# A graph attention kernel: the first stage's work is spread anew, and q's low half is cut strip by strip on GpSimd

## The reference, cut to what matters

```python
h = jnp.maximum(_layernorm(x), 0.0)                  # x: 4096 x 128
# layer 0
q, k, v = h @ Wq.T + bq, h @ Wk.T + bk, h @ Wv.T + bv
scores = jnp.where(adj > 0, q @ k.T / sqrt(128), -9e15)   # adj: 4096 x 4096 int32
x = x + elu(softmax(scores) @ v)
# layer 1
h = jnp.maximum(_layernorm(x), 0.0)
g = h @ W
e = leaky_relu((g @ a[:128])[:, None] + (g @ a[128:])[None, :], 0.01)
x = x + g + softmax(jnp.where(adj > 0, e, -9e15)) @ h
```

## Time and profile before

| | us |
|---|---|
| median of three executions | 794.09 |
| the profiled execution | 794.8 |
| its span | 793.0 |
| TensorE busy (matmuls) | 745.1 (94%) |
| VectorE | 582.4 (73%) |
| ScalarE | 560.0 (71%) |
| GpSimd | 365.7 (46%) |
| mean granted clock of TensorE | 0.974 |

### The profile page before, as it was taken

One profiled execution on the slowest core, in us unless ns is written; L12 is line 12 of the kernel. 1 busy time (PEld: TensorE's weight loads), 2 busy tenths in 40 slices (PEclk: granted clock), 3 DMA queues, 4 the chain that ended last, 5 costly groups with the idle time before them and its releaser, 6 DMA issues. The chain is left out here.

```text
span 793.0 us, 18058 instructions
## 1 busy us (share of the span) xinstructions
PE 745.1 (94%) x6229; PEld 629.7 (79%) x6229; DVE 582.4 (73%) x1231; ACT 560.0 (71%) x1095; POOL 365.7 (46%) x317
## 2 busy tenths in 40 slices
PE   4977999999999999999999998694999999999997
PEld 3555888888888888888888887473888888888886
DVE  4847788888788888888787886488674775685582
ACT  5936667676777768686777768484967977977911
POOL 1068587878878787878878772244000000000000
PEclk9989999999999999999999999788899999999999
DMA  6059888879787888978797842460133343333100
GB/s 225 1 183 255 265 200 242 237 211 230 214 259 201 257 219 234 239 209 233 211 256 205 254 118 41 96 132 0 32 72 82 89 76 83 88 83 89 36 10 12
DMA packets 155532, 122.47 MB, mean 154 GB/s; under 512 B 136545, under 2 KB 143201, under 8 KB 147297
## 3 DMA queue, kind: packets, MB, share of 16 engines
q1 hardware_dynamic: 154752, 121.66, 57.8%
q10 hardware_dynamic: 576, 0.26, 0.1%
q0 software_dynamic: 160, 0.00, 0.0%
HBM read 69.47 MB, written 18.87 MB: 111 GB/s over the span
## 5 line engine op out<-in xcount | busy, mean ns | idle before, releaser
L1333 PE MATMUL ps_x<-v,big 128*128 128x258 bf16 x2048 | 232.2, 275 | 2.3 <-issue 2.3
L1333 PEld LDWEIGHTS ps_x<-v,big 128*128 128x128 fp8e4 x2048 | 199.0, 98 | 32.6 <-issue 2.4
L679 DVE CUSTOM_DVE_ANT_0 scores<-ps_s,mask_neg 128x1024 f32<-128x1024 f32 x128 | 156.0, 1219 | 8.2 <-PE ps_s L766 8.2
L600 ACT ACTIVATE scores<-scores,neg_max 128x1024 f32<-128x1024 f32 x128 | 146.1, 1144 | 12.7 <-DVE neg_max L685 12.2
L537 POOL TENSOR_SCALAR mask_bytes<-adj_sb 128x2048 uint8<-128x2048 int32 x64 | 121.0, 1908 | 44.9 <-POOLq L79 39.9
L607 ACT ACTIVATE pT_high<-ps_t 128x512 bf16<-128x512 f32 x128 | 76.1, 595 | 91.4 <-PE ps_t L780 90.6
L874 ACT ACTIVATE big<-s_block,s_col 128x512 fp8e4<-128x512 f32 x224 | 139.6, 722 | 0.0
L698 DVE TENSOR_TENSOR low<-scores 128x1024 bf16<-128x1024 f32 x64 | 113.0, 1765 | 28.5 <-ACT scores L600 23.5
L552 POOL TENSOR_SCALAR mask_neg<-mask_bytes 128x2048 bf16<-128x2048 uint8 x64 | 126.7, 1979 | 5.4 <-POOL mask_bytes L537 0.4
L764 PE MATMUL ps_s<-k_hi,q_strip 128*128 128x512 f32 x256 | 113.1, 442 | 6.5 <-DVE row_max L679 4.2
L766 PE MATMUL ps_s<-k_hi,q_strip 128*128 128x512 f32 x256 | 102.2, 399 | 0.0
(11 more groups left out here) (139 smaller groups left out, 1059.2 us busy)
## 6 DMA issues: line engine op xcount, KB each, us to landing
adj_sb<-in_adj SPq DMA_DIRECT2D x64, 1024.0 KB, 6.4
mask_bytes_dram<-mask_bytes SPq DMA_DIRECT2D x32, 512.0 KB, 3.0
x_sb<-in_x SPq DMA_DIRECT2D x8, 256.0 KB, 6.0
out<-res SPq DMA_DIRECT2D x32, 64.0 KB, 1.5
lowT<-low SPq DMA_TRANSPOSE x64, 5.2
big<-mask_bytes_dram SPq DMA_TRANSPOSE x32, 4.5
raw_w<-in_L_gnn_Wq ACTq DMA_DIRECT2D x1, 64.0 KB, 3.4
raw_w<-in_L_gnn_Wk ACTq DMA_DIRECT2D x1, 64.0 KB, 4.2
```

The lines of the kernel that those rows point to most:

```text
L600: nc.scalar.activation(sc, sc, ACT.Exp, bias=neg_max[:, bn:bn + 1], accum_out=row_sum[:, bn, k:k + 1]).then_inc(exp_done, 1)
L679: nc.vector.tensor_tensor_reduce(out=scores[bn % 2][:, part(k)], in0=ps_s[k % 2][:], in1=mask[bn % 2][:, part(k)], scale=1.0, scalar=LOWES ...
L1333: last = nc.tensor.matmul(ps_x[b % 2][k][:], by_key_tile(m, t)[:, b], v1[k][:, t, :].bitcast(BF16), start=(t == 0), stop=(t == T - 1))
```

## The change

1. The first stage is a block of its own, no longer `norm_and_project`. GpSimd normalises three tiles of each chunk, ScalarE the fourth. Only k is split in high and low there; q becomes one f32 tile, `q_sb`. The first strips of q are cut in it, and GpSimd makes strip 0's bytes between the chunks and its mask behind them.
2. The v products, `hT` kept for them, move to the attention loop's block, ahead of period 0, in `ps_t` between the first scores of strips 0 and 1.
3. In the loop, ScalarE copies the high half of a strip of q (`q_high_strip`), and GpSimd subtracts it from `q_sb` for the low half (`q_low_strip`), behind `make_mask`. TensorE waits for both.

```diff
+            def q_high_strip(n, par):
+                src = bass.ds(n * D, D) if not isinstance(n, int) else slice(n * D, n * D + D)
+                nc.scalar.activation(q_strip[par][:, 0, :], q_sb[:, src], ACT.Copy).then_inc(q_ready, 1)
+
+            def q_low_strip(n, par):
+                src = bass.ds(n * D, D) if not isinstance(n, int) else slice(n * D, n * D + D)
+                nc.gpsimd.wait_ge(q_ready, n + 1)
+                if not isinstance(n, int):
+                    nc.gpsimd.sem_inc(pool_gate, 1)
+                nc.gpsimd.tensor_tensor(q_strip[par][:, 1, :], q_sb[:, src], q_strip[par][:, 0, :].bitcast(F32),
+                                        ALU.subtract).then_inc(q_low_ready, 1)
...
@@ GpSimd, first stage @@
+                    def normalise(c):
+                        pool.wait_ge(inverse_ready, c + 1)
+                        for t in range(4 * c, 4 * c + 3):
+                            last = nc.gpsimd.tensor_scalar(xc[:, t, :], x_sb[:, t, :], minus_mean[:, t:t + 1], rstd[:, t:t + 1],
+                                                           ALU.add, ALU.mult)
+                        last.then_inc(h_ready, 1)
+                    for c in range(NC):
+                        normalise(c)
+                        if c == 1:
+                            for par in range(2):
+                                q_low_strip(par, par)
+                        if 3 <= c < 7:
+                            k = c - 3
+                            pool.wait_ge(adj_in[k // 2], 16)
+                            last = bytes_piece(0, adj_sb[k // 2], k)
+                            if k % 2:
+                                last.then_inc(bytes_ready, 1)
+                    pool.wait_ge(bytes_ready, 2)
+                    for k in range(NP):
+                        last = mask_piece(0, k)
...
@@ ScalarE, first stage @@
+                    for c in range(NC):
+                        if c + 2 < NC:
+                            roots(c + 2)
+                        if c + 1 < NC:
+                            hT_out(c + 1)
...
+                        act.wait_ge(k_made, c + 1)
+                        nc.scalar.activation(k_hi[:, cols(c)], pk[c % 2][:], ACT.Identity, bias=bias[:, 1:2]).then_inc(k_high_out, 1)
+                        if c + 2 < NC:
+                            normalise(c + 2)
...
+                        act.wait_ge(q_made, c + 1)
+                        nc.scalar.activation(q_sb[:, cols(c)], pq[c % 2][:], ACT.Identity, bias=bias[:, 2:3]).then_inc(q_read, 1)
...
@@ VectorE, first stage @@
+                    for c in range(NC):
+                        if c + 2 < NC:
+                            inverse(c + 2)
+                        dve.wait_ge(k_high_out, c + 1)
+                        nc.vector.scalar_tensor_tensor(out=k_lo[:, cols(c)], in0=pk[c % 2][:], scalar=bias[:, 1:2],
...
+                        if c + 3 < NC:
+                            moments_of(c + 3)
...
@@ GpSimd, attention loop @@
-                    for b in range(3):
-                        make_bytes(0, b)
-                        if b < 2:
-                            make_mask(0, b)
+                    make_bytes(0, 1)
+                    make_mask(0, 1)
+                    make_bytes(0, 2)
 
                     def period(c, b):
                         if has(c, b, -2):
                             add_elu(4 * c + b - 2)
                         if has(c, b, 2):
                             make_mask(*at(c, b, 2))
+                            q_low_strip(4 * c + b + 2, b % 2)
                         if has(c, b, -1):
                             add_halves(4 * c + b - 1)
...
-                        nc.scalar.activation(q_strip[par][:, 0, :], q_hi[:, strip_cols(n)], ACT.Copy).then_inc(q_ready, 1)
-                        nc.scalar.activation(q_strip[par][:, 1, :], q_lo[:, strip_cols(n)], ACT.Copy).then_inc(q_ready, 1)
+                        q_high_strip(n, par)
...
@@ VectorE, attention loop @@
                     for k in range(NP):
                         add_mask(0, 0, k)
                     find_max(0, 0)
+                    for c in range(3):
+                        v_low(c)
                     add_mask(1, 1, 0)
+                    for c in range(3, 5):
+                        v_low(c)
                     low_part(0, 0, 0)
+                    v_low(5)
                     add_mask(1, 1, 1)
+                    for c in range(6, NC):
+                        v_low(c)
...
-                            pe.wait_ge(q_ready, 2 * n + 2)
+                            pe.wait_ge(q_ready, n + 1)
+                            pe.wait_ge(q_low_ready, n + 1)
...
@@ turn(s, b, i) @@
+                        if isinstance(s, int) and s == 0 and i < 3:
+                            pe.wait_ge(v_ready, (7, 8, 6)[i])
...
@@ TensorE, attention loop @@
                     for k in range(NP):
                         make_scores(0, 0, k)
+                    for c in range(3):
+                        v_product(c)
                     make_scores(1, 1, 0)
+                    for c in range(3, 6):
+                        v_product(c)
                     make_scores(1, 1, 1)
+                    for c in range(6, NC):
+                        v_product(c)
```

More of the change, by code:

```diff
@@ L89, in norm_and_project @@
         highs = sum(job[1] is not None for job in jobs)
-        bn, moments, root, rstd, shift = (stats[k] for k in ("bn", "moments", "root", "rstd", "shift"))
+        bn, moments, root, rstd = (stats[k] for k in ("bn", "moments", "root", "rstd"))
         @block.sync
@@ L171, in inverse @@
                 dve.wait_ge(root_ready, c + 1)
[L172 to L176, removed]
+                steps.do(nc.vector.reciprocal(rstd[:], root[:]))
             def normalise(c):
@@ L182, in normalise @@
                 last.then_inc(h_ready, 1)
[L184 to L195, removed]
+            all_moments()
+            inverse(0)
+            normalise(0)
+            normalise(1)
             for c in range(NC):
-                if x_in and c + 3 < NC:
-                    moments_of(c + 3)
-                if not x_in and c + 2 < NC:
+                if c + 2 < NC:
                     normalise(c + 2)
@@ L383, in k_product @@
-                def k_product(ps, c):
-                    return nc.tensor.matmul(ps[:], turned[1][:], hT[:, cols(c)], start=True, stop=True)
-                def k_high(ps, c):
-                    return nc.scalar.activation(k_hi[:, cols(c)], ps[:], ACT.Identity, bias=bias[:, 1:2])
-                def k_low(ps, c):
-                    return nc.vector.scalar_tensor_tensor(out=k_lo[:, cols(c)], in0=ps[:], scalar=bias[:, 1:2],
-                                                          in1=k_hi[:, cols(c)].bitcast(F32), op0=ALU.add, op1=ALU.subtract)
@@ L418, in build, with roots, hT_out @@
-            q_ready = sem("q_strip_ready")
-            s_ready, masked, mask_ready = sem("scores_ready"), sem("scores_masked"), sem("mask_ready")
+                    for i in (1, 0, 2, 3):
+                        act.dma_start(*weights[i]).then_inc(w_in[i], 16)
+                    def roots(c):
+                        act.wait_ge(var_ready, c + 1)
+                        nc.scalar.activation(root[:, tiles(c)], moments[:, tiles(c), 1], ACT.Sqrt, bias=eps[:]).then_inc(root_ready, 1)
+                    def hT_out(c):
+                        act.wait_ge(h_turned, c + 1)
+                        nc.scalar.activation(hT[:, cols(c)], pt[c % 2][:], ACT.Relu).then_inc(hT_ready, 1)
@@ L434, in build @@
             with ExitStack() as c2:
-                mask = [sb(c2, f"mask_neg{i}", [D, N], BF16) for i in range(2)]
                 scores = [sb(c2, f"scores{i}", [D, N], F32) for i in range(2)]
```

288 lines of the change are left out of this document (179 added, 109 removed).

## The result

| | before | after |
|---|---|---|
| median, us | 793.37 (789.1 to 796.37, 4 runs) | 838.31 (837.74 to 838.65, 4 runs) |
| after / before | 1 | 1.0572, 95% interval 1.0526 to 1.0617 |
| span of the profiled execution, us | 793.0 | 836.4 |
| mean granted clock | 0.974 | 0.983 |

The kernel became 5.7% slower; 838.3 us against a forecast of 835. The first view to take up is the timeline of a strip in the hardware loop, the same piece that the earlier trace rows shows of before. Columns: start, duration, engine, line, operation, and in brackets the idle time before it with what ended it.

What follows compares the result with a forecast made beforehand. In the attention loop TensorE alone was taken to set the end. From 794.8 us, -5 for the start and +45.3 for the loop's waits gave 835.1, predicted as 835, range 822 to 856.

Steps and rivals of the forecast that it cites:

- One wait per strip, behind two mask pieces: Attention loop: TensorE's scores wait for GpSimd's low half of q, 28 waits, 1.56 + 27 x 1.62 = 45.3 us.
- The bounds of 39 to 53 us: Attention loop: range for the summed waits, from 1.4 to 1.9 us for one wait.
- The slow clock: Rival, attention loop: each gap drops TensorE's clock to 1.2 GHz, some 1.5 us in each of 28 strips, 877; chance 0.07.
- The collision: Attention loop: add_elu's third addition overlaps VectorE's low part, 0.9 us paid; rival that they separate, 809 us, chance 0.05.
- rule that GpSimd takes about twice as long as VectorE: Loop's low half of q: by this alone VectorE makes it 0.2 us sooner, the sum some 6 us lower.
- The start: First stage and attention's first strips together: -5 us, bounds -9 to +3.
- the gap of chunk 2: First stage: GpSimd waits between chunks 1 and 2 for ScalarE's first q strips; no separate price.
- The mask made early: First stage: the first strip's mask on GpSimd, 3.88 us, is hidden; without cover up to 3.9 us.
- The first turn comes at about the same time as now: Attention's strip 0: VectorE's lost 6.17 us idle is filled by eight v parts, some 5.5 us, which turns wait for.
- the upper bound: Start: 5.5 us of v parts all on the path less 3 gained, +3 us.
- What is late next is DMA: Attention's first strips: TensorE idles 3.27 us for lowT; transfers starting 4 to 5 us sooner shrink or remove it.
- the start term: The -5 us of the start, said to cover the low half for s = 0 and 1, where no add_elu precedes the mask.

Runs made afterwards that it cites:

- e1: After kernel with two lines swapped, GpSimd making the low half of q ahead of the two mask pieces; 787.8 us, ratio 0.9928.
- e2: Kernel before, with only the low half of q from strip 2 on moved to GpSimd behind the mask; 846.42 us, ratio 1.0668.
- e6: After kernel with GpSimd's order turned round: whole mask, then low half of q, then add_elu; 788.35 us, ratio 0.9946.
- e3: After kernel with a second low half of q made into a spare tile ahead of the real one; 857.53 us, ratio 1.0814.
- e5: After kernel with the low half of q made by VectorE, behind the first pT low part, not by GpSimd; 786.48 us, ratio 0.9915.
- e8: e1 with VectorE's moments ahead of k's low part, and the first two q strips' low halves behind chunk 2, not chunk 1; 781.75 us, ratio 0.986.
- e11: e9 without the v products and their parts, two copies of x standing in for v; 772.89 us, ratio 0.975.
- e9: e8 with strip 1's adjacency asked for in the first stage, not after its end; 779.43 us, ratio 0.9836.

## Why the prediction was right, point by point

**One wait per strip, behind two mask pieces.** Right in mechanism, place and count: 28 waits, released by GpSimd's low half, and the strips absorb none of them, since the chain from att_exp to TensorE closes a loop. In e1 two swapped lines remove it, in e2 it comes back alone, and e6 shows that the loop is closed by att_exp.

**Its size.** Forecast 45.3 us, measured 1.4 + 48.0 = 49.4. The strips' spacing in the hardware loop is (485.31 - 127.90) / 23 = 15.54 us, 1.80 over 13.74 and not 1.62. The term that was mis-sized is the hop from GpSimd's last instruction to TensorE: taken as 0.06 us, it is 0.23 (267.46 to 267.69), and 0.23 to 0.28 in all 24 waits of the hardware loop. In the strips written out it is 0.10 (97.01 to 97.11); there the idle time is 1.38 to 1.46 us, and two such strips are 15.31 and 15.28 us apart, under the forecast. The bounds of 39 to 53 us held both.

**The rivals.** The slow clock did not come (1.00 in both stretches), though e3 shows that it began only 0.4 us of gap away, and cost there 0.8 to 1.6 us in each of 8 strips, not 1.5 in each of 28. The collision stayed (1.39 us at 261.57), as argued. In e6 it falls on another of the additions (1.45) and on the mask (4.73), so it moves with the order and is not lost. The Trainium skill's rule that GpSimd takes about twice as long as VectorE ("GPSIMD Engine Reference", "Performance versus the Vector engine") would have made the loss 6 us smaller on VectorE. The same subtraction takes 0.28 us there for 0.46 on GpSimd (e5 at 103.00; after at 267.00), so the rule is near. Measured, the loss vanishes on VectorE, but it vanishes on GpSimd too, one place earlier in the queue. The place decided.

**The start.** Forecast -5 us, measured -6.1: the sum came out, its terms did not come the way that was forecast. The first scores start 3.24 us sooner (41.78, before 45.02), forecast as 3. The chunk took 3.37 us against 3.5; the gap of chunk 2 (3.43 us of TensorE) was named without a price, and e8 gives it one, 4.5 us at the first scores. The mask made early was hidden, as said. But by strip 2's first scores this head start is spent: they start at 68.07, its wait of 1.46 included, where they started at 68.18. What is gained is gained between there and strip 3's. Before:

```profile
68.18 0.48 PE L764 MATMUL ps_s<-k_hi,q_strip 128*128 128x512 f32 x1
...
79.00:80.00 1.00, 1.00 (x8) 0.93 (x6) 0.96 (x4) 0.00 (x0) 1.00 (x1) 0.50 1.03 262
...
88.07 0.47 PE L764 MATMUL ps_s<-k_hi,q_strip 128*128 128x512 f32 x1
```

After:

```profile
81.79 0.48 PE L870 MATMUL ps_s<-k_hi,q_strip 128*128 128x512 f32 x1
```

The stretch takes 13.72 us (68.07 to 81.79) where it took 19.89. Before, it holds the wait of 3.27 us for lowT and, right behind that, some 6.5 us at a granted clock of 0.50; both are gone, and what each gave was not measured apart.

Three sentences of the prediction failed here. "The first turn comes at about the same time as now": it comes at 60.58, before at 59.18, and it waits for a v part in VectorE's queue:

```profile
60.58 0.63 PE L888 MATMUL ps_t<-ident,scores 128*128 128x128 f32 x4 [2.08 <-DVE v_parts L811]
```

That the turns wait for the v parts was in the prediction, but was priced in the upper bound alone, not in the -5; by e11 the v work costs 6.5 us. "What is late next is DMA": TensorE's wait for lowT is gone, and by e9 the load of strip 1's adjacency is not on the path either. And for s = 0 and 1 the start term was to cover the low half, since no add_elu stands ahead of the mask; for s = 1 that holds, but for s = 0 the two mask pieces alone, released by the late bytes and slowed to 4.64 us, make it 1.46 us late (68.07). Without that wait the start saves 8.0 us in e5, where the clock stayed up (strip 4's first scores at 93.83), and 6.4 in e1, where it fell once.

So the two errors, +4.1 in the loop and -1.1 at the start, leave 838.3 against 835. The loop, 45.3 us of the forecast, was right for its reasons. That the start came within 1.1 us was luck: the v work was taken as nothing, and lowT and the clock as less than the 6.2 us that they gave together.

## What to carry to other kernels

Before an instruction is given to an engine with much idle time, write down that engine's queue over one period and find where its idle time lies: if it lies in one wait, work behind that wait is on the chain that the wait began, however idle the engine is on average. Then compare the end of the new instruction with the moment at which its reader asks; 0.4 us to spare costs nothing, 1.4 us too late costs 1.4 us in each period. If the place is wrong, move the instruction a few lines up before changing its engine.

## What the runs showed of the hardware

- The hop from the end of GpSimd's instruction to the waiting matmul is 0.23 to 0.28 us inside the hardware loop and 0.10 us in the strips written out, in the after kernel, e2 and e3 alike. TensorE waits for the same semaphores in both, so their number doesn't explain it; in the loop the addresses and the values waited for come from registers, and no run tells what of that costs the 0.15 us.
- The two low halves that GpSimd makes in a row in e3 start 0.41 us apart, though each is shown as 0.45.
- After gaps of 1.92 to 2.06 us the granted clock fell to 0.50 in 8 of 19 strips that are alike (e3); after 28 gaps of 1.4 to 1.7 us in none (after). The same wait of 2.08 us in the first strip brought it down in e1 and not in the after kernel.
- Page part 5 puts VectorE's low part at a mean of 1265 ns in the after kernel and 1920 ns in e1, with the same shape. In e1 one of the two low parts of a strip takes 1.21 us and the other 2.85 (at 250.94, while GpSimd makes mask bytes, 248.97 to 252.72); in the after kernel, where GpSimd's bytes end at 272.13, the one at 272.18 takes 1.23. None of it reached the end.
